# Products of constants on TensorE in the heads of two tiled attentions, of a cross-attention loop and of two expert stages

## The chip, the cores and the metric

One core of a Trainium2 chip. The metric is the device time of one launch in microseconds (us), the median of several runs. PE is TensorE, DVE is VectorE, ACT is ScalarE, POOL is GpSimd, SP is the engine that issues most transfers.

## The reference

A two-layer decoder on x of 1024 tokens by 128 features, batch 1, float32. Layer 0: attention with distance weights, a GELU MLP over a context of 6404 rows, an expert MLP with top-1 routing. Layer 1: rotary attention, cross-attention to the same 6404 rows, and a last block that holds another attention and another expert MLP. The outer skeleton, with `_layernorm` after each residual sum:

```python
x = _layernorm(x + _L0_attn_ref(x, ...))
x = _layernorm(x + _L0_xattn_ref(x, ctx_1024, ctx_1024))
x = _layernorm(x + _L0_ffn_ref(x, ...))                     # 8 experts
x = _layernorm(x + _L1_attn_ref(x, Wq, Wk, Wv, Wo))         # rotary, 16 heads of 64, softmax
x = _layernorm(x + _L1_xattn_ref(ctx_1024, ctx_1024, x, mask, 16, ...))
x = _layernorm(x + _L1_ffn_ref(x, ...))                     # inside: x + _msa(...), then x + _moe_mlp(...)

# _msa and the rotary attention end in the same way:
attn = jax.nn.softmax(scores, axis=-1)      # over all 1024 tokens
y = attn @ v
return y.reshape(b, n, d) @ w_proj
# _moe_mlp, and _L0_ffn_ref with relu and gates:
logits = xf @ gate_w + gate_b
h = gelu(einsum('td,edh->teh', xf, w1)); y = einsum('teh,ehd->ted', h, w2)
```

## The kernel before

Activations stand transposed, features on the 128 partitions, tokens along the free axis (`x` is 128x1024). PSUM is one tensor `banks` of 8 banks of 512 float32 columns. The program is a row of blocks, one for each stage, with a barrier between blocks; inside a block every engine has its own hand-written order and waits on semaphores. Nothing is planned by a scheduler.

`layer_norm` ends each stage. Its last PE instructions are six products of the constants `center` and `onesd` (`turn_over(6)` inside it, line 543), whose results nobody reads. The trace shows each float32 product as two PE instructions (two passes over the same columns), each with its own weight load (rows of the engine PEld); a bfloat16 product is one.

`routed_mlp` (expert stages `moe0` and `moe1`): after the barrier PE waits for `s_small` (a transfer of the router's weights), makes 8 logits products (line 834), then `hidden` products of expert 0 (line 842) as soon as its weights have landed.

`tiled_attention` (called as `rotat` with `RotaryOperands` and as `lastat` with `PlainOperands`) finds a row maximum first. A *look* (line 1276) is a bfloat16 product of 32 rows by 512 columns into one of two banks; DVE reduces it to a maximum (line 1487). `free` makes look k wait until DVE has finished look k-2. Before the first pass stand 32 looks for pass 0. In `lastat` they come in one run behind `tensor_first` (the q, k and v products, lines 1142 and 1145). In `rotat` they come 8 at a time, each 8 behind a rotary `product` (lines 1049 and 1054). Then `turn(0)` (line 1286) transposes the maxima, DVE writes them to `F`, and the passes begin: scores (line 1297, four products of 32 rows side by side), exponentials on ACT, values (line 1316), with the looks of the next pass in between.

`cross_main`: PE makes q (1748), the first halves of two `piece` products (1673), then waits for `s_kh` and `s_qa`, the second halves (1675) and the other half of q (1755). DVE splits the pieces into `crat_Q` (lines 1799 to 1807). Then the loop starts: three score products (1690) per unit, one exponential of 128x1536 on ACT (1790), eight value instructions (1706). Twice in a pass, `extra` puts another piece between units; its second half stands behind score products without a wait of its own:

```python
for e, p, at in (("a", 0, 20), ("b", 1, 32)):
    if (ps, e) in X and u in (at, at + 4):
        if u == at:
            pe.wait_ge(s_xc, X[ps, e])
        of = piece(spare(ps), 2 * ((ps + 1) // 2) + p, (ps + 1) % 2, (u - at) // 4)
```

Of the kernel before, what the change touches and what calls it, by code (L numbers as in the profile page):

```python
# [68 lines left out]
class Count:  # L69
# [9 lines left out]
    def done(self):  # L79

        self.eng.wait_ge(self.sem, self.base + self.n)


def half(ap, h):
# [700 lines left out]
def routed_mlp(nc, PS, name, x, ident, w, func, weighted, early=None):  # L785
# [6 lines left out]
    with ExitStack() as ctx:  # L792
# [23 lines left out]
        with nc.Block() as block:  # L816
# [12 lines left out]
            @block.tensor  # L829
            def _(pe):  # L830
                pe.sem_inc(s_y, 2)
                pe.wait_ge(s_small, 16)
                for t in range(NT):
                    last = pe.matmul(PS[:, 6, t * EXPERTS:(t + 1) * EXPERTS], x[:, t * P:(t + 1) * P], wr,
                                     start=True, stop=True, skip_group_check=True)
                last.then_inc(s_logits, 1)

                def hidden(e, k, f):

                    pe.wait_ge(s_a, e * FC + f + 1)  # L840
                    for h in range(2):
                        last = pe.matmul(PS[:, 2 * (f % 2) + h, :], W[:, k, f * P:(f + 1) * P], half(x, h),
                                         start=True, stop=True)
                    last.then_inc(s_h, 1)

                def back(e, k, f):
                    pe.wait_ge(s_a, e * FC + f + 3)
                    if f == 0:

                        pe.wait_ge(s_comb, e * NT + NT)  # L850
                    for t in range(NT):
                        last = pe.matmul(PS[:, Y[k] + t // 4, (t % 4) * P:(t % 4 + 1) * P],  # L852
                                         A[:, f % 2, t * P:(t + 1) * P], W[:, k, FF + f * P:FF + (f + 1) * P],
                                         start=(f == 0 and t % 4 == 0), stop=(f == FC - 1), skip_group_check=True)
                    last.then_inc(s_y, 1)

                def expert(e, k, first=False):
                    pe.wait_ge(s_w[k], ((e - k) // 2 + 1) * 16 if isinstance(e, int) else (e - k) * 8 + 16)
                    for f in range(FC):
                        hidden(e, k, f)  # L860
                        if f:
                            back(e, k, f - 1)
                        elif not first:
                            back(e - 1, 1 - k, FC - 1)


                expert(0, 0, True)
                pe.wait_ge(s_gates, 1)
                expert(1, 1)
                with pe.Fori(1, EXPERTS // 2) as i:  # L870
                    expert(2 * i, 0)
                    expert(2 * i + 1, 1)
                back(EXPERTS - 1, 1, FC - 1)
                if weighted:
                    for t in range(NT):
                        last = pe.transpose(PS[0:EXPERTS, 2 + t // 4, (t % 4) * P:(t % 4 + 1) * P], G[:, t, :], ident[:, :])
                    last.then_inc(s_gt, 1)

                pe.wait_ge(s_comb, EXPERTS * NT + NT)
                for t in range(NT):  # L880
                    last = pe.matmul(PS[:, t // 4, (t % 4) * P:(t % 4 + 1) * P], acc[:, t, :], ident[:, :],
                                     start=(t % 4 == 0), stop=not weighted, skip_group_check=True)
                if weighted:
                    pe.wait_ge(s_gtc, 1)
                    for h in range(2):
                        pe.matmul(PS[:, h, :], b2, half(GT, h), start=False, stop=True, skip_group_check=True)
# [133 lines left out]
class RotaryOperands:  # L1020
# [4 lines left out]
    ORDER = [o for g in range(GROUPS) for o in (g, GROUPS + g)]  # L1025
    AHEAD = 4
    STEPS = 2 * GROUPS - AHEAD

    def __init__(self, nc, ctx, PS, x, pre, Q, K, Qb, Kb, V, wo, early):
        n = Names(nc, ctx, "rotop")  # L1030
# [39 lines left out]
    def tensor(self, pe, i):  # L1070
        self.product(pe, self.AHEAD + i)

    def tensor_done(self, pe):
        pe.wait_ge(self.s_cast, 2 * GROUPS)
        pe.wait_ge(self.s_vals, NT)
        pe.wait_ge(self.s_wo, 1)
# [32 lines left out]
class PlainOperands:  # L1109
# [2 lines left out]


    STEPS = 1

    def __init__(self, nc, ctx, PS, x, weights, Q, K, Qb, Kb, vst, wproj, sel, rows):
        n = Names(nc, ctx, "lastop")
# [32 lines left out]
    def tensor(self, pe, i):  # L1150
        pass

    def tensor_done(self, pe):
        pe.wait_ge(self.s_low, GROUPS + 1)
        pe.wait_ge(self.s_k, GROUPS)
        pe.wait_ge(self.s_vals, 1)
# [26 lines left out]
        pool.memset(self.vst.rearrange("q a b c -> q (a b c)"), 1.0).then_inc(self.s_set, 1)  # L1183


def tiled_attention(nc, PS, name, operands, Qs, Ks, Qbs, Kbs, stationary, scale, wo, H, ident, sel=None, rows=None, ES=None,
                    spare=None):

# [30 lines left out]
    with ExitStack() as ctx:  # L1221
# [36 lines left out]
        with nc.Block() as block:  # L1258
# [5 lines left out]
            def _(pe):  # L1264
# [15 lines left out]
                def turn(ps):  # L1280

                    pe.wait_ge(s_mb, ps + 1)
                    free(turn_slot(ps))
                    for t in range(4):
                        of = mb[:, t, :] if pairs else mb[:, ps // 2, t, :]
                        last = pe.transpose(turned_bank(ps)[:, t * P:(t + 1) * P], of, ident[:, :])
                    last.then_inc(s_mu, 1)
# [67 lines left out]
                for i in range(operands.STEPS):  # L1355
                    operands.tensor(pe, i)
                    for at in range(i * each, (i + 1) * each):
                        look(at)
                turn(0)
                operands.tensor_done(pe)  # L1360
                for ps in range(PASSES):
# [230 lines left out]
    KEYS = 16 * 2 * len(CROSS_BLOCKS)  # L1592


def cross_main(nc, PS, name, x, cross, tiles, On, qf, flag):

# [31 lines left out]
    with ExitStack() as ctx:  # L1630
# [22 lines left out]
        with nc.Block() as block:  # L1653
# [15 lines left out]
            def _(pe):  # L1669
# [78 lines left out]
                pe.matmul(PS[:, 6, :], tiles.wq[:, :], half(x, 0), start=True, stop=True).then_inc(s_qn, 1)  # L1748
                for p in range(2):
                    piece(4 + p, p, 0, 0)  # L1750
                pe.wait_ge(s_kh, 2)
                pe.wait_ge(s_qa, 1)
                for p in range(2):
# [1 line left out]
                pe.matmul(PS[:, 7, :], tiles.wq[:, :], half(x, 1), start=True, stop=True).then_inc(s_qn, 1)  # L1755

                pe.wait_ge(s_set, 2)
                gone = 0
                for ps in range(PASSES):
                    for u in range(UNITS):  # L1760
# [329 lines left out]
                dve.tensor_copy(HT, PS[:, 2:4, :].rearrange("q a b -> q (a b)")).then_inc(s_ht, 1)  # L2090


def cross_attention(nc, PS, x, a, cross, tiles, On, ident):

    with ExitStack() as ctx:
        n = Names(nc, ctx, "cross")
        flag = n.sb("flag", [1, 1], I32)
        qf = tiles.arena.take([T])
        w = {"mask": a["mask"], "k": cross["k"], "q": nc.dram_tensor("cross_q", (3, P, T), BF16).ap()}
        cross_main(nc, PS, "crat", x, cross, tiles, On, qf, flag)  # L2100
        cross_general(nc, PS, "crgen", w, cross["V"], tiles, qf, On, ident, flag)


def last_block(nc, PS, x, a, center, onesd, ident, identb, cols):

    with ExitStack() as ctx:
        n = Names(nc, ctx, "last")
        normed = n.sb("normed", [P, T])
        xa = n.sb("xa", [P, T])
        xxa = n.sb("xxa", [P, T])  # L2110
        with ExitStack() as inner:
            m = Names(nc, inner, "lastat")
            Q = m.sb("Q", [P, 1, T])
            K = m.sb("K", [P, GROUPS, T])
            Qb = m.sb("Qb", [P, 1, T], BF16)
            Kb = m.sb("Kb", [P, GROUPS, T], BF16)
            vst = m.sb("vst", [P, NT, HEADS, 32])
            H = m.sb("H", [P, GROUPS, T])
            wproj = m.sb("wproj", [P, HALF])
            sel = m.sb("sel", [P, P])  # L2120
            rows = m.sb("rows", [P, 3, GROUPS])
            operands = PlainOperands(nc, inner, PS, normed, a, Q, K, Qb, Kb, vst, wproj, sel, rows)
            layer_norm(nc, PS, "lastn1", center, onesd, x, normed, scale=cols[:, 2:3], shift=cols[:, 3:4], early=operands)
            tiled_attention(nc, PS, "lastat", operands, lambda g: Q[:, 0, :], lambda g: K[:, g, :], lambda g: Qb[:, 0, :],
                            lambda g: Kb[:, g, :], lambda c, g, r: vst[:, c, 4 * r + g, :], 1.0 / float(np.sqrt(D8)), wproj, H,
                            ident, sel=sel, rows=rows)
        layer_norm(nc, PS, "lastn2", center, onesd, x, normed, Y=4, keep=xa, also=(xxa, x), scale=cols[:, 4:5], shift=cols[:, 5:6])
        routed_mlp(nc, PS, "moe1", normed, ident, {"small": a["small1"], "experts": a["experts1"]}, ACT.Gelu_apprx_tanh, False)
        layer_norm(nc, PS, "ln6", center, onesd, xxa, x, Y=0)
def decoder(nc, a, out):  # L2130
    with ExitStack() as ctx:
# [32 lines left out]
        with ExitStack() as mid:  # L2164
# [5 lines left out]
            with ExitStack() as inner:  # L2170
# [11 lines left out]
                ES = tiles.K[:, 2:4, :].rearrange("q a t -> q (a t)").bitcast(F32)[:, 0:8 * HALF]  # L2182
                tiled_attention(nc, PS, "rotat", operands, lambda g: wide[:, g, :], lambda g: K[:, g, :], lambda g: Qb[:, g, :],
                                lambda g: Kb[:, g, :],
                                lambda c, g, r: V[:, c, g * P + 32 * r:g * P + 32 * r + 32], 0.5, wo, wide, identb,
                                ES=ES.rearrange("q (a b c) -> q a b c", b=4, c=HALF), spare=tail)
            layer_norm(nc, PS, "ln4", center, onesd, x, x, Y=4)
            cross_attention(nc, PS, x, a, cross, tiles, wide, ident)
        layer_norm(nc, PS, "ln5", center, onesd, x, x, Y=6, bias=cols[:, 1:2])
        last_block(nc, PS, x, a, center, onesd, ident, identb, cols)  # L2190
        with nc.Block() as block:
# [153 lines left out]
```

## Time and profile before

| | |
|---|---|
| median of 3 runs | 2423.93 us (2423.44 to 2425.89) |
| the profiled execution | 2420.78 us, its span 2419.1 us |
| PE busy | 2226.4 us (92%) |
| ACT busy | 1636.6 us (68%) |
| DVE busy | 953.6 us (39%) |
| mean granted clock of PE | 0.96 |

PEclk, the granted clock, is a share of full speed: 1.00 is 2.4 GHz, 0.50 is 1.2 GHz. A row of a timeline holds its start, the time from the first start to the last end of the instructions merged in it, engine, line, operation, output<-inputs, rows*columns of the weights and the moving operand, the count, and in brackets the idle time before it with what ended it. A row of a table by stretches holds start:end, length, PE busy (instructions), PEclk, DMA share, GB/s. A matmul's duration holds some 0.17 us in which the next one already runs, so the distance between starts tells the pace.

### The profile page before, as it was taken

To read this page: it belongs to the slowest core of one execution; us is meant where nothing else is said; L and a number is where in the kernel's file an instruction comes from. 1 tells how busy PE (TensorE), PEld (TensorE's weight loads), DVE (VectorE), ACT (ScalarE), POOL (GpSimd) and SP (SyncE) were. 2 spreads that over 40 slices of the span, in tenths; PEclk is the share of its full clock that TensorE was granted. 3 is DMA by queue.
4 is the path that set the end of the run, shared out by engine and by line. 5 is a ranking of instruction groups with operands and counts; after the bars stand their busy time and mean duration, and the time that the engine had idled before them with its cause. 6 is when DMAs were issued, how large, how long until landed. Compare 5 with 4: busy or idle time off the path is not lost. (4 is left out here: it accounts for less than half of the span.)

```text
span 2419.1 us, 30487 instructions
## 1 busy us (share of the span) xinstructions
PE 2226.4 (92%) x12198; PEld 774.0 (32%) x12198; DVE 953.6 (39%) x1490; ACT 1636.6 (68%) x1296; POOL 476.0 (20%) x254
## 2 busy tenths in 40 slices
PE   6899999789989987999899999999999977999898
PEld 2333333234446642222211111111111122222466
DVE  5766776325541156666211111110111115886111
ACT  1999999623332223555599999999999964566433
POOL 0567777201000024666300000000000000000000
PEclk9899999889999998999999999999999996999999
DMA  1000000046544002000100010010000000000010
GB/s 43 5 9 5 5 1 1 0 158 215 193 148 187 26 0 71 1 1 1 21 26 1 1 43 1 1 43 1 1 1 1 1 1 9 1 1 1 21 35 26
DMA packets 29134, 79.01 MB, mean 33 GB/s; under 512 B 3600, under 2 KB 18976, under 8 KB 26928
## 3 DMA queue, kind: packets, MB, share of 16 engines
q1 hardware_dynamic: 15176, 30.98, 4.2%
q0 software_dynamic: 4384, 29.56, 3.5%
q10 hardware_dynamic: 9448, 16.70, 1.9%
q8 instruction: 90, 1.47, 0.3%
q14 instruction: 36, 0.29, 0.0%
HBM read 71.68 MB, written 5.59 MB: 32 GB/s over the span
## 5 line engine op out<-in xcount | busy, mean ns | idle before, releaser
L1790 ACT ACTIVATE crat_E<-banks 128x1536 f32<-128x1536 f32 x544 | 749.4, 1461 | 19.2 <-PE banks L1690 5.2
L1706 PE MATMUL banks<-crat_E,crat_vst 128*32 128x512 f32 x3264 | 435.4, 606 | 0.2 <-ACT crat_E L1790 0.2
L1690 PE MATMUL banks<-crat_Q,mid_arena 52*128 52x512 bf16 x1632 | 328.9, 385 | 21.3 <-ACT crat_E L1790 17.0
L1817 DVE COPY crat_vst<-all_crossV 128x96 f32<-128x96 f32 x136 | 34.3, 253 | 639.2 <-PE banks L1706 639.0
L462 POOL TENSOR_TENSOR dist_wsum<-dist_wsum,dist_D 128x1024 f32<-128x1024 f32 x88 | 208.0, 2363 | 7.8
L1421 ACT ACTIVATE rotat_E<-banks 128x1024 f32<-128x1024 f32 x128 | 124.0, 1021 | 116.4 <-PE banks L1305 116.2
L1690 PEld LDWEIGHTS banks<-crat_Q,mid_arena 52*128 52x128 bf16 x1632 | 60.3, 94 | 441.3 <-ACT crat_E L1790 315.2
L344 DVE TENSOR_SCALAR dist_D<-banks,dist_k 128x512 f32<-128x512 f32 x256 | 178.5, 746 | 52.0 <-PE banks L217 52.0
L1487 DVE TENSOR_REDUCE rotat_mx<-banks 128x1 f32<-128x512 f32 x256 | 163.2, 685 | 70.2 <-PE banks L1276 69.0
L1421 ACT ACTIVATE lastat_E<-banks 128x1024 f32<-128x1024 f32 x128 | 123.9, 1020 | 87.2 <-PE banks L1297 87.2
L1487 DVE TENSOR_REDUCE lastat_mx<-banks 128x1 f32<-128x512 f32 x256 | 163.3, 685 | 37.9 <-PE banks L1276 36.0
L1433 POOL MEMSET lastat_mb<- 128x2048 f32 x1 | 1.8, 1804 | 806.6 <-POOLq L63 806.6
L1469 POOL TENSOR_TENSOR mid_arena<-rotat_E 128x2048 f32<-128x2048 f32 x31 | 140.3, 4527 | 89.5 <-ACT rotat_E L1421 86.2
L212 PE MATMUL banks<-dist_Q,dist_K 64*128 64x512 f32 x512 | 144.6, 641 | 7.1 <-DVE dist_V L332 2.3
L755 ACT ACTIVATE mlp_A<-banks 128x1024 f32<-128x1024 f32 x51 | 52.2, 1023 | 135.7 <-PE banks L648 135.7
L852 PEld LDWEIGHTS banks<-moe_W,moe_A 128*128 128x128 f32 x1024 | 123.0, 192 | 45.0 <-issue 26.3
L852 PE MATMUL banks<-moe_W,moe_A 128*128 128x128 f32 x1024 | 125.8, 277 | 10.3 <-DVE moe_acc L954 10.3
L228 PE MATMUL banks<-dist_D,dist_V 128*64 128x512 f32 x512 | 122.9, 599 | 0.0
L1706 PEld LDWEIGHTS banks<-crat_E,crat_vst 128*32 128x32 f32 x3264 | 64.5, 108 | 174.5 <-issue 162.5
L954 DVE SCALAR_TENSOR_TENSOR moe_acc<-banks,moe_G,moe_acc 128x128 f32<-128x128 f32 x128 | 34.5, 342 | 210.7 <-PE banks L852 210.7
L405 ACT ACTIVATE dist_D<-dist_D 128x4096 f32<-128x4096 f32 x28 | 99.6, 3609 | 26.2 <-DVE dist_D L344 26.1
L648 PE MATMUL banks<-all_x,mlp_C 128*128 128x512 f32 x204 | 100.0, 615 | 10.2 <-DMA mlp_C<-in_ctx 10.2
(256 smaller groups left out, 2787.0 us busy)
## 6 DMA issues: line engine op xcount, KB each, us to landing
mlp_M<-in_mask POOLq DMA_DIRECT2D x28, 800.5 KB
mid_arena<-cross_k SPq DMA_DIRECT2D x42, 204.0 KB
moe_W<-in_experts SPq DMA_DIRECT2D x16, 512.0 KB, 3.5
mid_arena<-in_rot_tables ACTq DMA_DIRECT2D x8, 1024.0 KB, 19.3
mlp_C<-in_ctx SPq DMA_DIRECT2D x17, 384.0 KB, 4.6
cross_k<-mlp_kp ACTq DMA_DIRECT2D x17, 288.0 KB, 2.4
mlp_row<-in_mask POOLq DMA_DIRECT2D x1, 3202.0 KB, 12.5
mlp_M<-in_mask POOLq DMA_DIRECT2D x1, 3202.0 KB
```

Source lines behind the costliest of these rows:

```text
L212: pe.matmul(PS[:, at + s, :], K[D0 * s:D0 * s + D0, c * P:(c + 1) * P], Q[D0 * s:D0 * s + D0, h * HALF:(h + 1) * HALF], start=True, stop=F ...
L228: last = pe.matmul(PS[D0 * s:D0 * s + D0, 4 + h, :], V[:, p % 3, c, D0 * s:D0 * s + D0], D[:, p % 2, s, c, h * HALF:(h + 1) * HALF], start ...
L344: last = dve.tensor_scalar(D[:, b % 2, s, c, h * HALF:(h + 1) * HALF], of[:, s * HALF:(s + 1) * HALF], k2[:, c, s:s + 1], 0.0, ALU.add, AL ...
L462: pool.tensor_tensor(to, to, W[:, c, :], ALU.add).then_inc(s_add, 1)
L648: last = pe.matmul(PS[:, at + h, :], C[:, b, k, 0:P], half(x, h), start=True, stop=True)
L852: last = pe.matmul(PS[:, Y[k] + t // 4, (t % 4) * P:(t % 4 + 1) * P], A[:, f % 2, t * P:(t + 1) * P], W[:, k, FF + f * P:FF + (f + 1) * P] ...
L1421: act.activation(flat(E[:, at % NE, 2 * i:2 * i + 2, :]), flat(PS[:, S + 2 * i:S + 2 * i + 2, :]), ACT.Exp, scale=scale).then_inc(s_e, 1)
L1469: pool.tensor_tensor(flat(ES[:, (4 * ps + k) % 2, :, :]), flat(E[:, at % NE, :, :]), flat(E[:, (at + 1) % NE, :, :]), ALU.add).then_inc(s_ ...
L1487: dve.tensor_reduce(mx[:, t, r, kh:kh + 1], PS[:, MX + i % 2, :], AX.X, ALU.max).then_inc(s_mt, 1)
L1690: last = pe.matmul(PS[:, 3 * (at % 2) + k, :], K[s:s + ROWS, 2 * (g % 2) + pair, c * P:(c + 1) * P], Q[s:s + ROWS, 2 * g + pair, qh * HALF ...
L1706: last = pe.matmul(PS[32 * j:32 * j + 32, 6 + ps % 2, :], vst[:, (ps * STEPS + c // 3) % 3, c % 3, j, :], E[:, at // 3 % NE, at % 3, :], s ...
L1790: act.activation(flat(E[:, at % NE, :, :]), flat(PS[:, 3 * (at % 2):3 * (at % 2) + 3, :]), ACT.Exp, scale=CROSS_SCALE).then_inc(s_e, 1)
```

## The change

A new helper `turn_over` issues float32 products of a constant 128x128 matrix with itself, 128 columns into a PSUM bank that is free at that time. It is called at four kinds of places, on PE alone; no other engine's instructions change:

- `routed_mlp` (twice in the program): 8 products of `ident`, ahead of the wait for `s_small`.
- `tiled_attention`: one product of `center` behind each look from `QUIET` on, in the last step of the head. `QUIET` is 26 in `rotat` (looks 26 to 31: 6 products) and 4 in `lastat` (looks 4 to 31: 28 products). `tensor_quiet` is a wait that makes sure that the bank is free.
- `cross_main`: 4 products ahead of the waits for `s_kh` and `s_qa`, and 20 ahead of the loop.

```diff
+def turn_over(pe, to, of, times):
+
+    for _ in range(times):
+        pe.matmul(to[:, 0:P], of[:, :], of[:, :], start=True, stop=True)
...
                 pe.sem_inc(s_y, 2)
+                turn_over(pe, PS[:, Y[0], :], ident, 8)
                 pe.wait_ge(s_small, 16)
...
+    QUIET, FREE = 26, 0
...
+    def tensor_quiet(self, pe):
+        pe.wait_ge(self.s_ta, 4 * GROUPS)
...
+    QUIET, FREE = 4, 7
...
+    def tensor_quiet(self, pe):
+        pe.wait_ge(self.s_vals, 1)
...
                     operands.tensor(pe, i)
                     for at in range(i * each, (i + 1) * each):
                         look(at)
+                        if i == operands.STEPS - 1 and at >= operands.QUIET:
+                            if at == operands.QUIET:
+                                operands.tensor_quiet(pe)
+                            turn_over(pe, PS[:, operands.FREE, :], center, 1)
                 turn(0)
...
                 for p in range(2):
                     piece(4 + p, p, 0, 0)
+                turn_over(pe, PS[:, 0, :], center, 4)
                 pe.wait_ge(s_kh, 2)
                 pe.wait_ge(s_qa, 1)
...
                 pe.wait_ge(s_set, 2)
+                turn_over(pe, PS[:, 0, :], center, 20)
                 gone = 0
```

PE in the head of `lastat` before: the q and k products, the v products, 32 looks in one run, the transposes of `turn(0)`, the first scores. (In these lists a float32 product counts once.)

```order
L1142 MATMUL banks<-last_normed,lastop_W 128x512 x4
L1145 MATMUL banks<-lastop_W,last_normed 128x128 x8
L1276 MATMUL banks<-lastat_Kb,lastat_Qb 128x512 x32
L1286 MATMUL banks<-all_ident,lastat_mb 128x128 x4
L1297 MATMUL banks<-lastat_F,lastat_K 128x512 x4
```

The same place in the changed kernel, whose line numbers are 12 to 15 higher here:

```order
L1154 MATMUL banks<-last_normed,lastop_W 128x512 x4
L1157 MATMUL banks<-lastop_W,last_normed 128x128 x8
L1291 MATMUL banks<-lastat_Kb,lastat_Qb 128x512 x5
L87 MATMUL banks<-all_center 128x128
L1291 MATMUL banks<-lastat_Kb,lastat_Qb 128x512
L87 MATMUL banks<-all_center 128x128
L1291 MATMUL banks<-lastat_Kb,lastat_Qb 128x512
```

The one run of looks has become looks 0 to 4 and then product and look in turn, 28 products in all; in `rotat` the same happens behind look 26.

PE at the head of the cross loop before: q, pieces, pieces, q, then the first units of scores.

```order
L1748 MATMUL banks<-all_x,mid_arena 128x512
L1673 MATMUL banks<-all_x,mid_arena 128x512 x2
L1675 MATMUL banks<-crat_qa,mid_arena 128x512 x2
L1755 MATMUL banks<-all_x,mid_arena 128x512
L1690 MATMUL banks<-crat_Q,mid_arena 128x512 x12
```

The same place in the changed kernel:

```order
L1767 MATMUL banks<-all_x,mid_arena 128x512
L1692 MATMUL banks<-all_x,mid_arena 128x512 x2
L87 MATMUL banks<-all_center 128x128 x4
L1694 MATMUL banks<-crat_qa,mid_arena 128x512 x2
L1775 MATMUL banks<-all_x,mid_arena 128x512
L87 MATMUL banks<-all_center 128x128 x20
L1709 MATMUL banks<-crat_Q,mid_arena 128x512 x12
```

Four products now stand between the halves of the pieces, twenty between the last product of the head and the first scores; nothing else has moved.

## Rows read from the trace of the kernel before

**Rows 1.** Page: PE's granted clock, in tenths, in 40 equal slices.

```profile
PEclk9899999889999998999999999999999996999999
```

**Rows 2.** PE by stretches: start:end, length, busy (instructions), clock, DMA share, GB/s.

```profile
889.20:895.80 6.60, 6.39 (x9) 0.50 0.00 0
...
926.30:940.20 13.90, 12.16 (x58) 0.50 0.57 172
...
2014.80:2018.80 4.00, 1.71 (x8) 1.00 0.00 0
2019.00:2038.40 19.40, 16.00 (x27) 0.50 0.00 0
...
2275.00:2285.00 10.00, 8.80 (x23) 0.50 0.37 119
```

**Rows 3.** Timeline of PE, head of `lastat` and first pass.

```profile
2018.79 18.59 PE L1276 MATMUL banks<-lastat_Kb,lastat_Qb 32*128 32x512 bf16 x27 [0.21 <-DVE lastat_mx L1487]
2038.61 1.12 PE L1286 MATMUL banks<-all_ident,lastat_mb 128*128 128x128 f32 x4 [1.22 <-DVE lastat_mb L1500]
2040.66 2.09 PE L1297 MATMUL banks<-lastat_F,lastat_K 32*128 32x512 f32 x8 [0.93 <-DVE lastat_F L1510]
...
2055.44 1.24 PE L1297 MATMUL banks<-lastat_F,lastat_K 32*128 32x512 f32 x8
...
2059.12 1.24 PE L1297 MATMUL banks<-lastat_F,lastat_K 32*128 32x512 f32 x8
```

**Rows 4.** Timeline of PE: the last look before full products, at 1.2 GHz.

```profile
889.41 0.60 PE L1276 MATMUL banks<-rot_Kb,rot_Qb 32*128 32x512 bf16 x1 [0.21 <-DVE rotat_mx L1487]
```

**Rows 5.** Timeline of PE's weight loads (PEld), directly behind it.

```profile
889.95 0.50 PEld L1049 LDWEIGHTS banks<-all_x,mid_arena 128*128 128x128 f32 x2 [0.44 <-issue]
890.97 0.34 PEld L1049 LDWEIGHTS banks<-all_x,mid_arena 128*128 128x128 f32 x1 [0.52 <-issue]
891.82 0.34 PEld L1049 LDWEIGHTS banks<-all_x,mid_arena 128*128 128x128 f32 x1 [0.52 <-issue]
```

**Rows 6.** The same kind of place at 2.4 GHz: the look, then weight loads.

```profile
901.54 0.39 PE L1276 MATMUL banks<-rot_Kb,rot_Qb 32*128 32x512 bf16 x1 [0.21 <-DVE rotat_mx L1487]
...
901.86 0.30 PEld L1049 LDWEIGHTS banks<-all_x,mid_arena 128*128 128x128 f32 x2 [0.23 <-issue]
902.39 0.19 PEld L1049 LDWEIGHTS banks<-all_x,mid_arena 128*128 128x128 f32 x1 [0.24 <-issue]
```

**Rows 7.** Cross loop at 2.4 GHz, weight loads: 52-row scores, second half of a piece, scores.

```profile
1240.72 0.11 PEld L1690 LDWEIGHTS banks<-crat_Q,mid_arena 52*128 52x128 bf16 x3 [0.84 <-issue]
1241.26 0.30 PEld L1675 LDWEIGHTS banks<-crat_qa,mid_arena 128*128 128x128 f32 x2 [0.42 <-issue]
1242.31 0.11 PEld L1690 LDWEIGHTS banks<-crat_Q,mid_arena 52*128 52x128 bf16 x3 [0.76 <-issue]
```

**Rows 8.** Timeline of PE, end of the head of `rotat`.

```profile
926.21 0.61 PE L1286 MATMUL banks<-all_identb,rotat_mb 128*128 128x128 bf16 x4 [2.96 <-POOL rotat_mb L1452]
```

**Rows 9.** Timelines of PE, DVE and ACT, head of the cross loop.

```profile
1197.85 1.88 PE L1673 MATMUL banks<-all_x,mid_arena 128*128 128x512 f32 x4
1199.57 1.88 PE L1675 MATMUL banks<-crat_qa,mid_arena 128*128 128x512 f32 x4
...
1206.25 1.25 PE L1690 MATMUL banks<-crat_Q,mid_arena 52*128 52x512 bf16 x6 [3.94 <-DVE crat_Q L1807]
...
1200.63 0.75 DVE L1799 TENSOR_SCALAR crat_p<-banks,mid_arena 128x512 bf16<-128x512 f32 x1 [2.01 <-PE banks L1675]
...
1213.66 1.45 ACT L1790 ACTIVATE crat_E<-banks 128x1536 f32<-128x1536 f32 x1 [1.12 <-PE banks L1690]
```

**Rows 10.** Timelines of PE, heads of `moe0` and `moe1`.

```profile
726.19 6.60 PE L842 MATMUL banks<-all_x,moe_W 128*128 128x512 f32 x8 [0.66 <-DMA moe_W<-in_experts]
...
2276.20 3.58 PE L834 MATMUL banks<-moe_small,last_normed 128*128 128x8 f32 x16 [4.49 <-DMA moe_small<-in_small]
...
2279.63 6.41 PE L842 MATMUL banks<-last_normed,moe_W 128*128 128x512 f32 x8
```

More of the change, by code:

```diff
@@ L1183, in gpsimd, with tiled_attention @@
         pool.memset(self.vst.rearrange("q a b c -> q (a b c)"), 1.0).then_inc(self.s_set, 1)
-def tiled_attention(nc, PS, name, operands, Qs, Ks, Qbs, Kbs, stationary, scale, wo, H, ident, sel=None, rows=None, ES=None,
-                    spare=None):
+def tiled_attention(nc, PS, name, operands, Qs, Ks, Qbs, Kbs, stationary, scale, wo, H, ident, center, sel=None, rows=None,
+                    ES=None, spare=None):
     PASSES = 2 * GROUPS
@@ L1592, with cross_main @@
     KEYS = 16 * 2 * len(CROSS_BLOCKS)
-def cross_main(nc, PS, name, x, cross, tiles, On, qf, flag):
+def cross_main(nc, PS, name, x, cross, tiles, On, qf, flag, center):
     PASSES = 2 * GROUPS
@@ L2090, in _, with cross_attention @@
                 dve.tensor_copy(HT, PS[:, 2:4, :].rearrange("q a b -> q (a b)")).then_inc(s_ht, 1)
-def cross_attention(nc, PS, x, a, cross, tiles, On, ident):
+def cross_attention(nc, PS, x, a, cross, tiles, On, ident, center):
     with ExitStack() as ctx:
@@ L2099, in cross_attention @@
         w = {"mask": a["mask"], "k": cross["k"], "q": nc.dram_tensor("cross_q", (3, P, T), BF16).ap()}
-        cross_main(nc, PS, "crat", x, cross, tiles, On, qf, flag)
+        cross_main(nc, PS, "crat", x, cross, tiles, On, qf, flag, center)
         cross_general(nc, PS, "crgen", w, cross["V"], tiles, qf, On, ident, flag)
@@ L2125, in last_block @@
                             lambda g: Kb[:, g, :], lambda c, g, r: vst[:, c, 4 * r + g, :], 1.0 / float(np.sqrt(D8)), wproj, H,
-                            ident, sel=sel, rows=rows)
+                            ident, center, sel=sel, rows=rows)
         layer_norm(nc, PS, "lastn2", center, onesd, x, normed, Y=4, keep=xa, also=(xxa, x), scale=cols[:, 4:5], shift=cols[:, 5:6])
@@ L2184, in decoder @@
                                 lambda g: Kb[:, g, :],
-                                lambda c, g, r: V[:, c, g * P + 32 * r:g * P + 32 * r + 32], 0.5, wo, wide, identb,
+                                lambda c, g, r: V[:, c, g * P + 32 * r:g * P + 32 * r + 32], 0.5, wo, wide, identb, center,
                                 ES=ES.rearrange("q (a b c) -> q a b c", b=4, c=HALF), spare=tail)
             layer_norm(nc, PS, "ln4", center, onesd, x, x, Y=4)
-            cross_attention(nc, PS, x, a, cross, tiles, wide, ident)
+            cross_attention(nc, PS, x, a, cross, tiles, wide, ident, center)
         layer_norm(nc, PS, "ln5", center, onesd, x, x, Y=6, bias=cols[:, 1:2])
```

## The prediction

> **What bounds the kernel now.** I read the granted clock of the page first. PE runs at full clock nearly everywhere, and the tenths below 8 stand in a few slices only [rows 1]. So a change that issues products nobody needs can help only in the heads of stages, where the clock is low, and can hurt where PE is waited for. I then cut the heads into stretches of constant clock. The longest at 1.2 GHz is in `lastat`: 19.4 us of looks and 14.4 us behind them [rows 3]. The looks alone keep PE busy for 16.0 of 19.4 us, and the clock does not rise; in the 4 us before, with 1.71 us busy, it was still full. By contrast 6.6 us of full products (128 rows) were enough to bring it back in `rotat` [rows 2].
>
> What sets the end in the head of `lastat` is one chain: look, reduction, look, and after the 32nd `turn(0)` and the first scores. The 27 looks from 2018.79 take 18.59 us, so one comes each (18.59 - 0.60) / 26 = 0.69 us, and each waits for DVE [rows 3]. At 2.4 GHz a look and the next full product start 0.32 us apart (901.54 to 901.86) and at 1.2 GHz 0.54 us (889.41 to 889.95) [rows 4 to 6]. PE has 0.69 - 0.54 = 0.15 us to spare in each look. That is the room for a product of constants at 1.2 GHz.
>
> **What one product of constants costs.** It is two passes of 128 columns. A pass of 512 columns takes (1199.57 - 1197.85) / 4 = 0.43 us at 2.4 GHz [rows 9] and 891.82 - 890.97 = 0.85 us at 1.2 GHz [rows 5], so one of 128 takes 0.11 and 0.21 us: 0.22 and 0.43 us for a product among full products. Between looks more is paid. The first full pass behind a look takes 890.97 - 889.95 = 1.02 us at 1.2 GHz, 0.17 more than the next [rows 5], and 902.39 - 901.86 = 0.53 at 2.4 GHz, 0.10 more [rows 6]: its weights are loaded while nothing runs. The way back costs again: two passes from 1241.26 to the next scores' load at 1242.31 are 1.05 us = 0.10 + 2 x 0.43 + 0.09 [rows 7]. Might the load be hidden where no semaphore holds it? The second half of a piece in the cross loop has no wait, and its load still begins only 0.54 us behind that of the scores ahead of it, about when they are over [rows 7]. So I price it as exposed. A look and a product then take 0.32 + 0.10 + 0.22 + 0.09 = 0.73 us at 2.4 GHz and 0.54 + 0.17 + 0.43 + 0.09 = 1.23 us at 1.2 GHz. Each is more than DVE's pace, so PE becomes the bound of these looks at either clock.
>
> The Trainium skill ("TensorE: Matmul & The Clock Gate", section on what each phase of a matmul is for) says that PE pulls weight loads ahead of matmuls that are still running. By that rule a product would cost its 0.43 us alone; that would be the second rival below. The load at 1241.26 disagrees.
>
> **The sum**, part by part.
>
> (a) `lastat`. The products start behind look 4, at about 2018.4. The clock is full in 2014.8 to 2018.8 and low from 2019.0 on [rows 2]; half a microsecond of products does not stop that fall, since what has emptied the engine lies before it. Then looks 5 to 31 run at 1.2 GHz with a product behind each. Does the mix bring the clock back? Full products alone did. The mix of 32-row scores, looks and values in 926.3 to 940.2 left it low for 13.9 us with 12.16 us busy [rows 2]. In the new mix all rows are at work for 0.43 of 1.23 us, so I take it to be nearer to the second. Cost: 26 x (1.23 - 0.69) = +14.0 us, all on the path, since DVE waits for each look, `turn(0)` for the last maximum, and the first scores for `turn(0)`. The last product ends inside the wait of 1.22 us ahead of the transposes [rows 3]. The bounds of one step are 0 (hidden in the 0.15 us) and 0.54.
>
> (b) `rotat`. Five steps between looks 26 and 31 at full clock go from 0.60 (0.39 + 0.21 idle [rows 6]) to 0.73: +0.7 us, and the last look may meet the low clock: +0.2. PE then waits 2.96 us for POOL in any case [rows 8], so the products can't carry the clock into the first scores. +0.9 us.
>
> (c) Cross. The waits for `s_kh` and `s_qa` cost nothing today: the second halves follow the first at once [rows 9]. So 4 x 0.22 = +0.87 us goes in front of them, DVE, which waits for them at 1200.63, starts later, and so do the scores at 1206.25. The other 20 take 4.4 us behind a q product that ends near 1199.57 + 6 x 0.43 = 1202.15; they fit in a wait of 3.94 us plus the 0.87 shifted [rows 9] but for the change of form: +0.3. In return the clock may now be full when the scores begin. ACT, which sets the loop's pace, lost 1.12 us there waiting for PE [rows 9]. Between +1.2 and +0.1; I take +0.7.
>
> (d) `moe1`. Eight products from about 2274.3 (my estimate of the block's start) run into the fall of the clock that stands before 2275.0 [rows 2]: three at 0.22 and five at 0.43 us end near 2277.0, 0.8 us behind the 2276.20 at which the router's weights are there [rows 10]. All that follows until the clock rises is at half speed, and work that moves past the rise takes half as long, so half of it stays: +0.4. In `moe0` the first `hidden` product waits for a transfer until 726.19 [rows 10]; what is saved or lost ahead of it is hidden: 0, and were it not hidden, a saving of some 1.7 us, half of the 3.5 us of logits.
>
> Sum: 14.0 + 0.9 + 0.7 + 0.4 = +16.0 us. The profiled execution took 2420.78 us and so becomes 2436.8. The median of the runs is 3.15 us above it, and I carry that over: 2423.93 + 16.0 = 2439.9, **2440 us**.
>
> **The rivals.**
>
> *The clock goes up in the looks of `lastat`* (faster). If the products between looks keep or bring back 2.4 GHz, looks come each 0.73 us: 26 x 0.04 = +1.0. The first passes gain: three steps of a pass take 2055.44 - 2040.66 = 14.8 us now, where the next one takes 3.68 [rows 3]; three at that pace save 3.7. With luck in `moe1` too (half of 3.4 us of logits and half of the 5.5 us behind them, -4.5) and in the cross head (+0.1), and (b): 1.0 - 3.7 - 4.5 + 0.1 + 0.9 = -6.2, 2418 us. The sign turns at 12 slow steps of 0.50 us with the luck in `moe1`, and at about 1 without it. For it: full products do raise it. Against it: it must rise from 1.2 GHz, where the exposed loads leave the array idle more than at 2.4. The Trainium skill (same page, section on HAM oscillation) advises to leave PE no long gaps; by that rule this case would be the likely one. The looks, 16.0 of 19.4 us busy at 1.2 GHz [rows 2], show that a busy engine alone is not enough. Chance 0.12.
>
> *The weight load of the product hides behind the look.* Then a step is 0.43 + 0.43 = 0.85 us at 1.2 GHz, 26 x 0.16 = +4.2, with the rest +6.2: 2430 us. Chance 0.10.
>
> *A mixture*: the clock falls, comes back midway through the looks, and half of the slow steps are paid: +7, less 3.7 and some luck in the heads: about +2, 2426 us. This is also what the change doing little would look like. Chance 0.12.
>
> *The forecast*: 0.66, with a range of its own from 2434 to 2446: the way back to a look at 1.2 GHz is taken from a row at 2.4 GHz and may be 0.05 more or less (1.3 us), the cross loop gives 0.6 either way, `moe1` may save 4.5, and the clock's steps fall elsewhere in each run.
>
> **How the numbers follow.** A measurement tells this kernel from itself by about 0.2%, 4.8 us. Slower by more: all of the forecast, the second rival and a quarter of the mixture: 0.79. Within it: the rest of the mixture and the slow side of the first rival: 0.13. Faster: 0.08. The range goes from 2426 to 2446: it leaves out the first rival, half of the mixture and the outer ends of the forecast.
>
> **What the changed profile would show.** Looks of `lastat` from 4 to 31 about 1.23 us apart, with the clock at 0.50, DVE idle between its reductions, and scores some 14 us later after the v products. In `rotat` the last six looks 0.73 apart and the wait before `turn(0)` still there. In the cross head, `L1799` some 0.9 us later after the q product, and the gap of ACT of 1.12 us gone or not. In `moe1` logits a little behind their transfer. I am wrong if the looks come faster than 0.9 us apart, or if the clock is at 1.00 between looks 10 and 31.

## The result, and the profile after

| | before | changed |
|---|---|---|
| median of 7 runs | 2423.44 us (2420.92 to 2425.89) | 2434.47 us (2429.69 to 2443.17) |
| ratio | | 1.0049, interval 1.0034 to 1.0063 |
| the profiled execution | 2420.78 us | 2443.17 us |

The change costs 0.49%, by the ratio 0.0049 x 2423.44 = +11.9 us (+8.2 to +15.3). The forecast was +16.0 and 2440; the time is within its range and its sign is right. The profiled execution of the changed kernel happens to be the longest of its seven, so its total must not be compared with that of before; a second set of runs further down has a profile near the median.

The page of the changed kernel, its span, engines and granted clock:

```profile
span 2441.5 us, 30783 instructions
PE 2260.3 (93%) x12346; PEld 799.6 (33%) x12346; DVE 955.0 (39%) x1490; ACT 1637.3 (67%) x1296; POOL 476.4 (20%) x254
PEclk9899999899989987999999999999999995999899
```

PE is busier and the kernel is slower: a first sign that the added busy time stands on the path. The deep slice near the end reads 5 where it read 6 in [rows 1]. That is the head of `lastat`. PE there, by stretches:

```profile
2017.40:2024.10 6.70, 4.83 (x25) 1.00 0.00 0
2024.20:2059.80 35.60, 35.41 (x85) 0.50 0.00 0
```

PE is busy in 35.41 of 35.60 us, where it was busy in 16.00 of 19.40 us [rows 2], and the clock stays at 0.50, 1.2 GHz. Nearly no idle time is left, and it does not rise. The timeline of PE there:

```profile
2024.54 0.60 PE L1291 MATMUL banks<-lastat_Kb,lastat_Qb 32*128 32x512 bf16 x1 [0.19 <-DVE lastat_mx L1506]
2025.07 0.80 PE L87 MATMUL banks<-all_center 128*128 128x128 f32 x2
2025.80 0.60 PE L1291 MATMUL banks<-lastat_Kb,lastat_Qb 32*128 32x512 bf16 x1
2026.33 0.80 PE L87 MATMUL banks<-all_center 128*128 128x128 f32 x2
2027.06 0.60 PE L1291 MATMUL banks<-lastat_Kb,lastat_Qb 32*128 32x512 bf16 x1
...
2058.56 0.60 PE L1291 MATMUL banks<-lastat_Kb,lastat_Qb 32*128 32x512 bf16 x1
2059.09 0.80 PE L87 MATMUL banks<-all_center 128*128 128x128 f32 x2
2060.39 1.12 PE L1301 MATMUL banks<-all_ident,lastat_mb 128*128 128x128 f32 x4 [0.50 <-DVE lastat_mb L1519]
```

From 2025.80 to 2058.56 a look comes each (2058.56 - 2025.80) / 26 = 1.26 us, against 0.69 before [rows 3]. The looks' brackets are gone: they wait for DVE no more. DVE now waits for them:

```profile
2040.30 0.69 DVE L1506 TENSOR_REDUCE lastat_mx<-banks 128x1 f32<-128x512 f32 x1 [0.57 <-PE banks L1291]
```

And the loads, by which one step can be split:

```profile
2025.80 0.10 PEld L1291 LDWEIGHTS banks<-lastat_Kb,lastat_Qb 32*128 32x128 bf16 x1 [0.23 <-issue]
2026.33 0.50 PEld L87 LDWEIGHTS banks<-all_center 128*128 128x128 f32 x2 [0.44 <-issue]
2027.06 0.10 PEld L1291 LDWEIGHTS banks<-lastat_Kb,lastat_Qb 32*128 32x128 bf16 x1 [0.23 <-issue]
```

The look takes 2026.33 - 2025.80 = 0.53 us until the product's load can begin, and load, two passes and the way back take 2027.06 - 2026.33 = 0.73 us. Forecast were 0.54 and 0.17 + 0.43 + 0.09 = 0.69.

The head of the cross loop, PE and then ACT:

```profile
1204.37 1.88 PE L1692 MATMUL banks<-all_x,mid_arena 128*128 128x512 f32 x4
1206.08 1.05 PE L87 MATMUL banks<-all_center 128*128 128x128 f32 x8
1206.97 1.88 PE L1694 MATMUL banks<-crat_qa,mid_arena 128*128 128x512 f32 x4
1208.69 1.02 PE L1775 MATMUL banks<-all_x,mid_arena 128*128 128x512 f32 x2
1209.55 4.63 PE L87 MATMUL banks<-all_center 128*128 128x128 f32 x40
1214.11 0.82 PE L1709 MATMUL banks<-crat_Q,mid_arena 52*128 52x512 bf16 x6
```

```profile
1214.75 5.48 ACT L1811 ACTIVATE crat_E<-banks 128x1536 f32<-128x1536 f32 x4 [4.40 <-PE banks L1709]
1220.62 1.45 ACT L1811 ACTIVATE crat_E<-banks 128x1536 f32<-128x1536 f32 x1 [0.39 <-PE banks L1709]
1222.88 8.35 ACT L1811 ACTIVATE crat_E<-banks 128x1536 f32<-128x1536 f32 x6 [0.82 <-PE banks L1709]
```

Four products take 1206.97 - 1206.08 = 0.89 us ahead of the waits, and the twenty end in the scores with no wait between them. The scores' idle time of 3.94 us [rows 9] is filled. ACT still loses 0.39 + 0.82 = 1.21 us in the loop's first units, so its gap of 1.12 us [rows 9] has not gone in this execution; in `again`, below, it has.

### The profile page after: what moved, and what is told of

It reads as the page before. It is cut to its first block and busy times, and to the rows that moved or that the text cites. A ratio compares the mean times of both kernels' runs of the same rounds, so it can differ in the third digit from the quotient of the medians.

```text
span 2441.5 us, 30783 instructions
## 1 busy us (share of the span) xinstructions
PE 2260.3 (93%) x12346; PEld 799.6 (33%) x12346; DVE 955.0 (39%) x1490; ACT 1637.3 (67%) x1296; POOL 476.4 (20%) x254
## 5 line engine op out<-in xcount | busy, mean ns | idle before, releaser
L859 PE MATMUL banks<-moe_W,moe_A 128*128 128x128 f32 x1024 | 125.7, 276 | 10.4 <-DVE moe_acc L961 10.4
L654 PE MATMUL banks<-all_x,mlp_C 128*128 128x512 f32 x204 | 99.9, 614 | 10.6 <-DMA mlp_C<-in_ctx 10.6
```

The source lines that it names most:

```text
L654: last = pe.matmul(PS[:, at + h, :], C[:, b, k, 0:P], half(x, h), start=True, stop=True)
```

## The experiments

Each ratio is against the kernel before on the same chip in the same set of runs. All edits only add or omit products whose results nobody reads. `strip_last` and `bf16_last` ran once each and have no ratio; their clock rows and steps are read, not their times.

**One part at a time.** Four kernels, each the kernel before with one of the changed kernel's parts.

```diff
 # last_only                                # QUIET 99 in rotat: no products there
-                turn_over(pe, PS[:, Y[0], :], ident, 8)
-    QUIET, FREE = 26, 0
+    QUIET, FREE = 99, 0
-                turn_over(pe, PS[:, 0, :], center, 4)
-                turn_over(pe, PS[:, 0, :], center, 20)
 # rot_only: QUIET 26 and 99; cross_only: 99 and 99, with the 4 and the 20
 # moe_only: 99 and 99, with the 8 in both expert stages
```

> Only the 28 products between the looks of lastat; all others left out. Priced step by step (theory 1: each slow step costs 1.26 - 0.69 us at 1.2 GHz, always): +14 to +16 us against the kernel before in every execution, spread like that of before (some 5 us). Theory 2 (the clock stays up or comes back between the looks in a part of the executions): executions from about 0 to +16 us, looks in the trace partly 0.74 us apart.

> Only the 6 products between the last looks of rotat's head. Theory 1: +0.7 to +1.5 us. Theory 2 (the 17 us longer stretch at 1.2 GHz behind this head in the changed kernel's trace is caused by these products): +4 to +5 us in most executions.

> Only the 4 and the 20 products in the head of the cross loop. Theory 1: first scores 1.2 us later after the head's first product, of which up to 1.1 us comes back when ACT no longer waits for PE in the fifth unit: 0 to +1.2 us. Theory 2 (the clock is saved for the loop): -1 us or better.

> Only the 8 products ahead of the router's weights in both expert stages. Theory 1: moe0 nothing, moe1 between +0.4 us (clock falls while they run) and -4.5 us (clock stays up through logits and first hidden products), so a mean of about -1 us and executions some 4 us apart. Theory 2 (they only delay): +0.4 us in every execution.

| | median us (runs) | ratio, interval | us |
|---|---|---|---|
| `last_only` | 2439.35 (5) | 1.0068, 1.0055 to 1.0081 | +16.5 |
| `rot_only` | 2420.23 (11) | 0.9992, 0.9983 to 1.0002 | -1.9 |
| `cross_only` | 2421.67 (11) | 1.0000, 0.9991 to 1.0009 | 0 |
| `moe_only` | 2422.19 (12) | 1.0002, 0.9992 to 1.0012 | +0.5 |

(The median of before here is 2422.78 us, and the last column is (ratio - 1) times it.) The whole loss is in `lastat`. `rot_only` came out below both of its theories (its interval goes from -4.1 to +0.5 us), which rules out the +4 to +5. `moe_only` separates neither of its two: its executions are 10.4 us apart, as those of the kernel before are (10.6). PE in the head of `last_only`, by stretches:

```profile
2021.20:2069.00 47.80, 44.66 (x127) 0.50 0.00 1
```

The kernel before spends 33.8 us at 1.2 GHz there (2019.00 to 2052.80), this one 47.80. The first passes pay as before.

**Is it the exposed load, and does the kind of product matter to the clock?** `strip_last` takes products of 32 rows, on the same strip of the array (32 of its rows) as the look ahead and so not on the strip of the next look; `bf16_last` takes one bfloat16 pass of 128 rows. Both have products in `lastat` alone.

```diff
 # strip_last, behind look `at`
-    turn_over(pe, PS[:, operands.FREE, :], center, 1)
+    r = at % 4
+    of = center[32 * r:32 * r + 32, :]
+    pe.matmul(PS[:, (0, 1, 6, 7)[r], 0:P], of, of, start=True, stop=True)
 # bf16_last
-    turn_over(pe, PS[:, operands.FREE, :], center, 1)
+    turn_over(pe, PS[:, operands.FREE, :], identb, 1)
```

> As the kernel with products in lastat alone, but each product takes 32 rows of center, in the same row group and therefore the same 32-row form as the look ahead of it (it reads a quarter of the rows; passes and columns are the same). Theory A (what makes a step dear is the change between the 32-row and the 128-row form, which leaves the weight load uncovered): step of a look at 1.2 GHz falls from 1.26 us to 0.43 + 0.43 = about 0.86 us, the head of lastat some 10 us shorter than with the full products. Theory B (each float32 product costs its loads wherever it stands): step stays at 1.1 to 1.26 us.

> As the kernel with products in lastat alone, but the constants are the bfloat16 identity: one pass of 128 columns instead of two of four times the length per column. Theory A (change of form is the larger part of the price): step at 1.2 GHz about 0.54 + 0.17 + 0.11 + 0.09 = 0.85 to 0.95 us, still above the 0.69 us without products. Theory B (the passes are the price): 0.69 us as before, hidden in the 0.15 us to spare.

PE in `strip_last`, timeline and a stretch:

```profile
2025.78 0.63 PE L1379 MATMUL banks<-all_center 32*128 32x128 f32 x2
2026.17 0.60 PE L1291 MATMUL banks<-lastat_Kb,lastat_Qb 32*128 32x512 bf16 x1
2026.57 0.42 PE L1379 MATMUL banks<-all_center 32*128 32x128 f32 x1
2026.77 0.60 PE L1291 MATMUL banks<-lastat_Kb,lastat_Qb 32*128 32x512 bf16 x1
```

```profile
2024.80:2044.00 19.20, 18.40 (x79) 0.50 0.01 1
```

The next look starts (2026.17, 2026.77) while products of another strip are still at work. The weight loads show a second difference: the product's load begins with the look ahead of it, where in the changed kernel it began 0.53 us behind the look's start:

```profile
2026.17 0.10 PEld L1291 LDWEIGHTS banks<-lastat_Kb,lastat_Qb 32*128 32x128 bf16 x1
2026.17 0.73 PEld L1379 LDWEIGHTS banks<-all_center 32*128 32x128 f32 x2
```

So products and looks overlap, and DVE's reductions stand in unbroken runs:

```profile
2025.42 6.25 DVE L1508 TENSOR_REDUCE lastat_mx<-banks 128x1 f32<-128x512 f32 x9
```

6.25 / 9 = 0.69 us for each look, as before. From look 0 to `turn(0)` it is 23.12 us (before 23.25, changed 38.68). So the same count of float32 products costs nothing when each has 32 rows and the next look uses another strip. How much of that is the load beside the look, and how much the free strip, this run does not tell apart. I had expected 0.86 us a step, and did not foresee this overlap. PE in `bf16_last`:

```profile
2025.66 0.60 PE L1290 MATMUL banks<-lastat_Kb,lastat_Qb 32*128 32x512 bf16 x1
2026.20 0.29 PE L87 MATMUL banks<-all_identb 128*128 128x128 bf16 x1
2026.42 0.60 PE L1290 MATMUL banks<-lastat_Kb,lastat_Qb 32*128 32x512 bf16 x1
```

```profile
2017.20:2037.80 20.60, 19.83 (x53) 0.50 0.00 1
```

A step is 0.76 us here: look to product 0.54, product to look 0.22. Less the 0.17 us in which the next one already runs, the look itself takes 0.60 - 0.17 = 0.43 us and the product 0.29 - 0.17 = 0.12, so each change of form still costs some 0.10 us. That lies between my two theories (0.85 at least, or 0.69 with nothing exposed), and look 0 to `turn(0)` takes 24.69 us, 1.4 more than before. Of the float32 product's 0.73 us its two passes are 0.43 and 0.30 are left over, where the bfloat16 one leaves 0.10. So the change between 32 and 128 rows is one part of the price, and the float32 product, whose two loads take 0.50 us together where the one of `bf16_last` takes 0.10, adds some 0.2 us to it. The clock stays at 0.50 in both, at 96% busy.

**Can any product of constants raise the clock in the looks?** `side` puts behind each look four bfloat16 products of 32 rows by 512 columns, one on each strip of rows, which run at the same time, and fills the waits around `turn(0)` with full products. It has none in the cross and expert heads. `beside_only` has the four alone, `fill_only` the fillings alone.

```diff
                     for at in range(i * each, (i + 1) * each):
                         look(at)
+                        if operands.beside(pe, i, at):     # from look 2 on
+                            for s in range(4):
+                                pe.matmul(PS[:, operands.BESIDE[s], :],
+                                          Qbs(0)[32 * s:32 * s + 32, 0:P],
+                                          Kbs(0)[32 * s:32 * s + 32, 0:HALF],
+                                          start=True, stop=True)
+                turn_over(pe, PS[:, operands.FREE, :], center, operands.FILL[0])  # 11 / 4
                 turn(0)
                 operands.tensor_done(pe)
+                turn_over(pe, PS[:, operands.FREE, :], center, operands.FILL[1])  # 0 / 3
 # and in lastat two full products ahead of look 0 and two ahead of look 2
```

> A version of the idea that keeps the form: no products in the expert stages and the cross head; in both attention heads, behind each look from the third of its group on, four bfloat16 products of 32 rows by 512 columns side by side in four banks instead of one float32 product; 11 and 4 full products of center ahead of turn(0), 3 behind it in lastat, 2 ahead of look 0 and 2 ahead of look 2 there. Theory A with the clock: looks stay 0.60 us apart, the clock stays at 2.4 GHz through the looks and the rotary products: rotat's head 4 to 7 us shorter, lastat's looks 2.4 us shorter, and up to 4 us in each first pass: -6 to -15 us against before. Rival (the clock falls all the same): at 1.2 GHz the four products lengthen each step of lastat to 0.86 us, +4 us there, and about 0 in rotat.

> Of the version with products side by side only the full products of center in the waits are kept: 11 ahead of turn(0) in rotat; in lastat 2 ahead of look 0, 2 ahead of look 2, 4 ahead of turn(0), 3 behind it. No product between looks. Theory A (the clock through the looks is kept by the products side by side): the clock falls in the looks as before, looks of lastat 0.69 us apart, heads as long as before, total within 3 us of before. Rival (filling the longer waits is enough): -5 us or better.

> Only the four products side by side behind looks, none of the fillings. Theory A: rotat's head keeps 2.4 GHz and is some 3 us shorter; in lastat the clock falls before look 2 as it does before, and then each step is 0.86 us instead of 0.69 at 1.2 GHz: its head +4 us. Together about 0. Rival (the fillings do nothing): as the full version, -8 us.

`side` takes 2413.46 us (8 runs; before 2423.20), ratio 0.9968 (0.9956 to 0.9980), -7.8 us. `fill_only` takes 2421.39 (12; before 2421.87), 0.9997 (0.9987 to 1.0007). `beside_only` takes 2416.29 (12), 0.9983 (0.9971 to 0.9995), -4.1 us (-7.0 to -1.2), which is neither of its two theories. PE in the looks of `side`, timeline, then stretches:

```profile
2014.84 0.38 PE L1301 MATMUL banks<-lastat_Kb,lastat_Qb 32*128 32x512 bf16 x1
2014.85 0.60 PE L1391 MATMUL banks<-lastat_Kb,lastat_Qb 32*128 32x512 bf16 x4
2015.44 0.39 PE L1301 MATMUL banks<-lastat_Kb,lastat_Qb 32*128 32x512 bf16 x1
```

```profile
885.00:906.50 21.50, 19.16 (x102) 1.00 0.00 0
906.60:913.40 6.80, 6.80 (x21) 0.50 0.01 2
...
2016.00:2036.20 20.20, 18.82 (x154) 1.00 0.01 2
2036.40:2043.00 6.60, 5.86 (x28) 0.50 0.00 0
```

The four start with the look and cost it nothing: a look comes each 0.60 us, and in `lastat` the clock is full from look 0 to `turn(0)`. It isn't held everywhere: in `rotat` of the same execution it fell at 906.6 us, amid such products, for 6.80 us. Stretches of `fill_only` and `beside_only`:

```profile
2023.30:2043.00 19.70, 17.57 (x41) 0.50 0.00 0
```

```profile
2016.10:2022.70 6.60, 6.60 (x50) 0.50 0.00 0
2022.90:2039.80 16.90, 13.76 (x111) 1.00 0.01 1
```

Here the same stretch exists at both levels. In `beside_only` the clock had fallen, and after 6.60 us of side-by-side products it was back; in none of the eleven traces without them does it rise between the looks of `lastat`. A look came each (2022.37 - 2016.21) / 9 = 0.68 us in that low stretch, from the starts in the trace, so the four cost nothing at 1.2 GHz either, where I had expected 0.86. From look 0 to `turn(0)` it is 20.21 us in `side`, 21.62 in `beside_only`, 23.10 in `fill_only`, against 23.25 before. The head of `rotat` is 59.55 us in `side`, 62.61 - 59.55 = 3.1 us shorter, where I had expected 4 to 7.

**The changed kernel again, and the cross head's twenty.** `again` repeats the changed kernel in a second set, to see how much of its long first profile belongs to it. `cross20` is the kernel before with the 20 alone; `side_heads` is `side` with the 8 of the expert stages and 18 ahead of the cross loop.

```diff
 # side_heads = side and:
+                turn_over(pe, PS[:, Y[0], :], ident, 8)
+                turn_over(pe, PS[:, 0, :], center, 18)
```

> The changed kernel once more, for a second trace and more times. If the 30.7 us at 1.2 GHz behind rotat's head in its first trace came from where the clock's steps fell in that execution, this trace has 17 us or less there and the stage from turn(0) to the last scores is back at about 251 us; if the products cause it, it is 255 us again. lastat's head from look 0 to turn(0) 38 us in either case. Median 2433 to 2438 us.

> The kernel before with only the 20 products ahead of the cross loop; the 4 ahead of the waits are left out. If the 4 cost 4 x 0.22 = 0.87 us on the path: from the head's first product to the first scores 9.8 us (10.68 with the 4, 9.33 without any), the loop behind it as with both, 764 to 765.7 us, so 1 us less than before in all. If the 4 are hidden: 10.5 us or more.

> The version with products side by side, and with it the 8 products in the expert stages and 18 (not 20, and not the 4 ahead of the waits) in the cross head. The parts add: -8 us as without them, about -1 us in the cross loop (ACT's gap gone, first scores not later), and 0 to -4.4 us in the second expert stage: median 1 to 2 us below the version without, lowest execution below 2407 us. Rival (these heads give nothing): the same as without, within 1 us.

`again`: 2431.26 us (7 runs; before 2423.20), 1.0049 (1.0031 to 1.0067), a little below the 2433 to 2438 expected. `cross20`: 2422.34 (12 runs; before 2421.87), 1.0003 (0.9994 to 1.0013). `side_heads`: 2409.14 (6 runs), 0.9950 (0.9933 to 0.9966), -12.1 us: the lowest of this study and faster than both kernels. Its interval overlaps that of `side`, so what its heads add is not shown by these times.

Stage lengths, worked out in each trace from the first starts of the instructions named (us; in `rotat` from its first product to `turn(0)`):

| | before | changed | `again` | `last_only` | `side_heads` |
|---|---|---|---|---|---|
| `lastat` look 0 to `turn(0)` | 23.25 | 38.68 | 37.94 | 37.94 | 20.21 |
| `rotat` head | 62.61 | 62.73 | 63.75 | 62.62 | 57.78 |
| `rotat` `turn(0)` to last scores | 251.21 | 255.48 | 250.65 | 251.38 | 252.47 |
| cross q to first scores | 9.33 | 10.68 | 10.68 | 9.33 | 9.34 |
| cross first scores to last values | 765.82 | 765.64 | 764.08 | 766.99 | 764.05 |
| last scores to `moe1` logits | 22.07 | 23.98 | 24.83 | 23.47 | 24.82 |
| `moe1` logits to hidden | 3.43 | 3.27 | 1.88 | 3.44 | 1.87 |
| `moe1` hidden, first to last | 117.94 | 117.98 | 115.23 | 117.77 | 115.24 |

The 4.3 us that the first profile has more in `rotat` behind `turn(0)` are not there in `again`, with the same code: they come from a low clock that lasted 30.5 us there, against 17.0 in `again`:

```profile
921.80:952.30 30.50, 24.97 (x108) 0.50 0.45 116
```

`cross20` has its first scores where I expected them if the four stand on the path, 9.79 us behind q. Its loop missed: 766.99 us and not 764 to 765.7, because the clock fell at 1208.8 us and ACT then lost 1.26 + 1.27 = 2.53 us. In `again` the clock stays full there and ACT loses nothing, 24 exponentials in one run:

```profile
1207.36 32.65 ACT L1811 ACTIVATE crat_E<-banks 128x1536 f32<-128x1536 f32 x24 [4.40 <-PE banks L1709]
```

PE at `moe1` in `again`, by stretches and its timeline:

```profile
2287.40:2290.50 3.10, 3.10 (x17) 0.50 0.85 259
2290.80:2300.00 9.20, 9.20 (x49) 1.00 0.09 34
```

```profile
2287.02 3.52 PE L87 MATMUL banks<-all_ident 128*128 128x128 f32 x16 [2.42 <-PEq L63]
```

Here the eight products run at 1.2 GHz and the clock is full when the logits begin. They cost 24.83 - 23.47 = 1.4 us against `last_only` and give back 1.56 and 2.54 us in the two rows below. In the changed kernel's first profile the same eight start at 2296.13, the clock falls at 2297.2, and it is still low when they end:

```profile
2297.20:2307.40 10.20, 10.20 (x32) 0.50 0.36 114
```

## Why the forecast was right, and where its terms were off

**(a) `lastat`, +14.0.** Right in mechanism and nearly in size. The products left DVE waiting 0.57 us for each look, and a step became 1.26 us instead of the forecast 1.23. Look 0 to `turn(0)` grew by 38.68 - 23.25 = 15.4 us in the first profile and by 14.7 in `again` and `last_only`. In the first profile the clock is low from look 4 on, and 27 steps of 1.26 - 0.69 = 0.57 make 15.4. In `last_only` it falls a look later, as this timeline of PE shows:

```profile
2020.44 0.49 PE L87 MATMUL banks<-all_center 128*128 128x128 f32 x2
2020.86 0.38 PE L1290 MATMUL banks<-lastat_Kb,lastat_Qb 32*128 32x512 bf16 x1
2021.17 0.80 PE L87 MATMUL banks<-all_center 128*128 128x128 f32 x2
2021.90 0.60 PE L1290 MATMUL banks<-lastat_Kb,lastat_Qb 32*128 32x512 bf16 x1
```

Looks at 2.4 GHz are (2020.44 - 2020.12) + (2020.86 - 2020.44) = 0.74 us apart there (the look before starts at 2020.12; forecast 0.73), one step takes 2021.90 - 2020.86 = 1.04, and 25 take 1.26: 0.14 + 0.35 + 25 x 0.57 = 14.7. The forecast's term was mis-sized by the 0.03 us of a step and by up to one step. `last_only` by itself costs +16.5 (+13.3 to +19.6), so this term alone holds the result. The clock step was right too: the products neither kept 2.4 GHz nor brought it back, and the rival in which they do is out.

The rival of the hidden load is refuted for this product: 1.26 us is not 0.85. The Trainium skill ("TensorE: Matmul & The Clock Gate", section on what each phase of a matmul is for) has weight loads pulled ahead of matmuls that run, where their row groups don't conflict or the load goes to the background buffer; the prediction left that condition out. In `strip_last` the trace agrees: the product's load begins with the look, at 2026.17. Behind the looks of the changed kernel and of `bf16_last` it doesn't happen: the load of 128 rows, float32 or bfloat16, begins 0.53 us behind the look's start. The advice of the Trainium skill to leave PE no long gaps (same page, section on HAM oscillation) isn't enough here: with 35.41 of 35.60 us busy the clock stayed at 1.2 GHz.

**(b) `rotat`, +0.9.** The head grew by 63.75 - 62.61 = 1.1 us in `again` and by as much in `rot_only` (63.77), near the forecast. But it grew by 0.1 in the first profile, and in `cross20`, which has none of these products, it took 61.26 us: where the clock falls moves this stage by more than the term. The whole of `rot_only` is -1.9 us with an interval from -4.1 to +0.5, so I cannot tell the term's effect on the kernel from nothing.

**(c) Cross, +0.7.** The delay was right: first scores 10.68 - 9.33 = 1.35 us later, of which the four cost 0.89 (forecast 0.87; in `cross20`, without them, first scores come 9.79 us behind q, so 10.68 - 9.79 = 0.89 too). The other 0.46 is the twenty: in `cross20` they take 1205.77 - 1201.21 = 4.56 us, where before 1206.25 - 1202.15 = 4.10 lay between the end of q and the scores. The prediction added the shifted 0.87 to that wait; it moves the end of q as well, and so makes no room. With eighteen (`side_heads`) first scores come at 9.34, as before. What the products give back depends on the execution. With both the four and the twenty the loop took 765.64 (first profile), 765.67 (`cross_only`) and 764.08 us (`again`); nine traces with no product there have 765.81 to 767.34. The part measures 0 (-2.2 to +2.2), which neither confirms nor contradicts +0.7. The twenty alone measure +0.7 (-1.5 to +3.1).

**(d) `moe1`, +0.4, or -4.5 with luck.** Both cases occur. Ten traces without the eight products have 3.43 or 3.44 us from logits to hidden and 117.64 to 118.14 in hidden. With them, two (`again`, `side_heads`) have 1.87 to 1.88 and 115.2, and two (first profile, `moe_only`) have 3.27 and 118.0 or 117.5: little saved. The logits start later in all four: 23.98 to 24.83 us behind the last scores, against 23.28 to 23.74 in eight of the ten. (The kernel before has 22.07, as its clock was full there for longer, so the 1.9 us between the first two columns is not the products' price.) Against `last_only`, `again` gains 1.56 + 2.54 - 1.36 = 2.7 us. I had the lucky case as a clock that never falls; in fact the products run at 1.2 GHz and are what is at work until it rises. `moe_only` measures +0.5 (-1.9 to +2.9), so no gain on the whole is shown. In `moe0` the forecast's 0 holds: from the last product of the layer norm ahead to the first hidden one it is 7.56 to 8.02 us in the four traces with the eight, and 7.66 to 8.04 in `before`, `last_only` and `cross20`.

**The sum.** The four parts apart give 16.5 - 1.9 + 0 + 0.5 = +15.1, the forecast 16.0, the whole change +11.9 (+8.2 to +15.3). Most of the 4 us between forecast and result would be covered by (d)'s lucky case and (c)'s low end together, which is what the trace of `again` shows. That is an argument from one trace, though: +16.0 lies 0.7 us above the interval, the intervals of the parts are wider than that, and how often each case occurs in the runs stays open.

## What to carry to other kernels

Before putting products nobody needs in a wait, ask which real instruction comes next and who waits for it: the room in a look was 0.15 us, and a product of 0.73 us went in. Busy time by itself is the wrong goal: full products in turn with the looks cost 0.57 us each and raised nothing, while 32-row products side by side on all strips stood in the looks' shadow (0.60 us a look) and mostly held the clock. In front of work that a transfer or a reduction holds for microseconds full products are cheap if they are no longer than the wait (twenty were 0.46 us too long, eighteen fitted), and in `moe1` they paid only in executions in which the clock rose behind them before that work began. Read such a gain from several traces: one stage of unchanged code differed here by 1 to 5 us between them.

## What the runs showed of the hardware that I had not expected

- A busy PE alone did not raise the clock. 99% busy (35.41 of 35.60 us) with looks and full products in turn stayed at 1.2 GHz, and so did 96% in `strip_last` and `bf16_last`; in `beside_only` it rose after 6.60 us of side-by-side products of four strips, and in `side` it stayed at 2.4 GHz from look 0 to `turn(0)` of `lastat`, 20.21 us. In `rotat` of `side` it fell all the same for 6.80 us. Which property of these products makes the difference, no run here varies alone.
- Products on other strips of rows than a running look overlap with it: 0.38 us for the look and 0.60 us for look and four products together, of which three begin within 0.01 us of it; the fourth, on the look's own strip, begins 0.23 us later.
- A float32 product behind a 32-row look costs 0.73 us at 1.2 GHz, a bfloat16 one of the same shape 0.22. Their passes are 0.43 and 0.12 us, so 0.30 and 0.10 us come on top. A 32-row float32 product, whose load ran beside the look, cost nothing.
- The clock falls and rises at other places in each execution of the same code: `rotat` behind `turn(0)` took 255.48 and 250.65 us in two executions of the changed kernel, about as much as what separates the forecast from the result.
